# Two stages of deformable convolution on one core: image rows in four quarters over 128 partitions, shifted copies made by DMA, and four gathered groups instead of five

## The reference

```
x = x + layer0(gn(x))        x = x + layer1(gn(x))      gn: 32 groups, so each channel of each image by its own mean and variance
layer0(v): offsets = conv3x3(v) (8 maps), logits = conv3x3(v) (4 maps), attn = softmax(logits)
           sampled_k = bilinear sample of v at (pixel + offset_k), k = 0..3
           y = proj(sum_k attn_k * sampled_k);  batch norm of y over both images;  gamma, beta;  GELU
layer1(v): offset = conv3x3(v) (18 maps), m = sigmoid(conv3x3(v)) (9 maps)
           sample v (padded by one) at the nine taps of a 3x3 kernel, each shifted by its own offset, times m
           out = conv over the nine taps (32 -> 32 channels)
```

## Time and profile before

| what | value |
|---|---|
| median of three runs | 551.7 us (552.7, 551.7, 546.88) |
| span of the profiled execution | 551.0 us |
| what lies around the span, to the median | 0.7 us |
| PE, DVE, POOL, ACT busy | 83%, 78%, 69%, 37% |
| start, to the first window tile weighted | 0 to 44.6 us |
| loop of layer zero | 44.6 to 157.8 us |
| from there to the first interpolation of layer one | 157.8 to 204.9 us |
| layer one | 204.9 to 551.0 us |

### The profile page before, as it was taken

How to read it: one execution, slowest core, us unless ns; L and a number is a source line. 1 busy time by engine, 2 the same in 40 slices (tenths; PEclk the granted TensorE clock), 3 DMA queues, 4 the chain that set the end, 5 groups by cost and what they waited for, 6 DMA issues and landing times.

```text
span 551.0 us, 10909 instructions
## 1 busy us (share of the span) xinstructions
PE 459.4 (83%) x3913; PEld 261.4 (47%) x3913; DVE 429.5 (78%) x934; ACT 206.5 (37%) x352; POOL 379.0 (69%) x356
## 2 busy tenths in 40 slices
PE   5848888996750767989999999999899998899884
PEld 2527556665530522445555555555444444444443
DVE  5995667997759766788888879898787887779672
ACT  2714546321248556652433332333133142232201
POOL 6067656788827466577777777777777777777772
PEclk9756878998995756999999999999999999989999
DMA  8569747869500491122223227512112211212211
GB/s 201 180 154 202 192 89 125 158 114 157 124 18 0 158 119 46 37 68 73 74 72 91 70 73 110 86 49 54 54 54 58 58 49 54 58 49 56 55 49 32
DMA packets 43093, 48.48 MB, mean 88 GB/s; under 512 B 24482, under 2 KB 33954, under 8 KB 42532
## 3 DMA queue, kind: packets, MB, share of 16 engines
q1 hardware_dynamic: 32148, 25.52, 22.7%
q0 software_dynamic: 10752, 22.04, 15.9%
q10 hardware_dynamic: 144, 0.24, 0.2%
HBM read 39.02 MB, written 8.75 MB: 87 GB/s over the span
## 4 chain that ended last, share of the span: by engine, by line
PE 35%; POOL 25%; issue 15%; DVE 8%; DMA 8%; ACT 6%; SPq 1%; POOLq 1%; DVEq 0%; ACTq 0%
POOL got L570 23%; PE ps_later L1193 4%; PE ps_pair L1193 4%; DMA got<-table,idx 4%; PE ps_x L1206 4%; PE ps_raw L1169 4%; ACT xn L654 3%; DMA raw<-in_x 3%; PE ps_raw L983 3%; PE ps_x L1216 2%; PE ps_o L996 2%; POOL xn L555 1%; PE ps_pair L1042 1%; PE ps_later L1020 1%; SPq L445 1%
## 5 line engine op out<-in xcount | busy, mean ns | idle before, releaser
L570 POOL DMA_INDIRECT got<-table,idx x336 | 352.4, 1049 | 143.8 <-issue 109.7
L1811 DVE TENSOR_TENSOR prod<-got,wgt 128x512 f32<-128x512 f32 x64 | 44.2, 690 | 30.2 <-DMA got<-table,idx 29.8
L1612 DVE TENSOR_TENSOR vprod<-ps_pair,rhat 128x704 f32<-128x704 f32 x64 | 56.8, 887 | 9.7 <-PE ps_pair L1193 9.3
L1206 PE MATMUL ps_x<-early,vprod 128*128 128x128 f32 x384 | 56.3, 284 | 1.0 <-DVE vlast L1623 0.6
L1612 DVE TENSOR_TENSOR vprod<-ps_later,rhat 128x704 f32<-128x704 f32 x64 | 56.5, 882 | 0.9 <-PE ps_later L1193 0.8
L1206 PEld LDWEIGHTS ps_x<-early,vprod 128*128 128x128 f32 x384 | 42.4, 145 | 30.6 <-issue 17.3
L1620 DVE TENSOR_TENSOR vprod<-vprod 128x640 f32<-128x640 f32 x64 | 52.8, 825 | 1.2
L1794 DVE TENSOR_TENSOR samples<-shared,vprod 128x800 f32<-128x800 f32 x44 | 43.0, 984 | 12.2 <-PE ps_pair L1042 4.9
L1216 PE MATMUL ps_x<-early,prod 128*128 128x128 f32 x256 | 39.3, 277 | 10.5 <-DVE prod L1811 10.3
L654 ACT ACTIVATE xn<-raw,aff 32x1472 f32<-32x1472 f32 (+6 forms) x24 | 43.0, 1802 | 13.6 <-DVE aff L1394 9.4
L1169 PE MATMUL ps_raw<-conv_out,later 128*128 128x512 f32 x64 | 39.7, 704 | 0.7 <-ACT shared L827 0.7
(11 more groups left out here) (204 smaller groups left out, 776.3 us busy)
## 6 DMA issues: line engine op xcount, KB each, us to landing
shared<-positions SPq DMA_DIRECT2D x22, 440.0 KB
got<-table,idx POOLq DMA_INDIRECT x336, 6.0
raw<-in_x SPq DMA_DIRECT2D x16, 256.0 KB, 10.1
table<-trow SPq DMA_DIRECT2D x16, 256.0 KB, 2.0
y<-table SPq DMA_DIRECT2D x4, 512.0 KB, 8.6
table<-trow SPq DMA_DIRECT2D x4, 504.0 KB
out<-ysumT SPq DMA_DIRECT2D x64, 16.0 KB
later<-in_later SPq DMA_DIRECT2D x1, 530.0 KB, 18.9
```

Of the source, the lines that this page charges most:

```text
L570: pool.indirect_dma_start(into[t][:, s * P:(s + 1) * P], None, tab, bass.IndirectOffsetOnAxis(ap=idx[:, slot, k:k + 1], axis=0),).then_inc ...
L1206: nc.tensor.matmul(bank[:, P:2 * P], vprod[:, t % 2, r, :], idn[:], start=(r == 0), stop=(r == HALF - 1), is_transpose=True)
L1612: nc.vector.tensor_tensor(dst, ps_dense[pair_number(0, t, pair) % 2][:].rearrange("p (d n) -> p d n", d=2)[:, :, 0:WROWS * C].rearrange("p ...
L1811: nc.vector.tensor_tensor(prod[:, t % 2, :].rearrange("p (k s c) -> p s k c", k=CORNERS, c=C), got[t].rearrange("p (s k c) -> p s k c", s= ...
```

## The change

`raw` now holds an image once: row quarter q (16 rows, and the row below it) on partitions 32q to 32q+31. The steps that follow from it:

- `load_x`: four transfers an image instead of eight. Statistics and the residual sum work on 128 partitions and 1024 columns an image; a matmul with a rotated identity (`combine`) brings the four quarters' statistics to every partition.
- `normalise` is one DVE instruction an image into `xq` (quarters, padded); 16 transfers of 32 partitions an image (`load_shifted`) make the four shifted copies in `xn`. The first rows of group 0 are written directly by ACT and DVE (`head`). The row above a quarter comes by a matmul (`turn_edge`, `normalise_edge`).
- Tables: four 128x128 transposes make one of 8 (layer zero) or 9 (layer one) pieces; the table of layer zero goes out in two sends, that of layer one in three and three small ones (image 1: nine and three).
- Layer zero gathers four groups (16 steps) and takes twelve as windows, three tiles a step. One PSUM bank each for the gathered and the window sums. `fold_y` adds into PSUM banks that hold four groups by quarter, with the bias put there by a matmul (`start_y`); the copies to `y0` are gone, statistics and GELU read PSUM. Four GELUs instead of sixteen.

The core of the diff:

```diff
-NGA = 5
+NGA = 4
+GATHERED = [(0, 2 * i) for i in range(NGA)]
-UNITS = [[(0, 5), (0, 6)], [(0, 7)], [(1, 0), (1, 1)], [(1, 2), (1, 3)], [(1, 4), (1, 5)], [(1, 6), (1, 7)]]
+UNITS = [[(0, 1), (0, 3)], [(0, 5), (0, 7)], [(1, 0), (1, 2)], [(1, 4), (1, 6)], [(1, 1), (1, 3)], [(1, 5), (1, 7)]]
-CONV_AT = {(0, 0): [5], (1, 0): [6], (1, 1): [7], (2, 0): [8], (3, 1): [9], (4, 1): [10], (5, 1): [11], (6, 1): [12],
-           (7, 1): [13], (9, 1): [14], (10, 1): [15]}
+CONV_AT = {(0, 0): [6], (0, 1): [7], (1, 0): [8], (2, 0): [9], (2, 1): [10], (5, 0): [11], (6, 0): [12], (6, 1): [13],
+           (8, 0): [14], (8, 1): [15]}
...
+            def load_shifted(b, q, skip=0):
+                for g in range(CORNERS):
+                    dy, dx = g // 2, g % 2
+                    n = (QROWS - skip) * WP - dx
+                    src, dst = (1 + skip) * WP + dx, (1 - dy + QROWS * q + skip) * WP
+                    sp.dma_start(xn[C * g:C * (g + 1), b, dst:dst + n],
+                                 xq[C * q:C * (q + 1), b, src:src + n]).then_inc(xn_in[b][q], 16)
...
+            for q in range(Q):
+                load_shifted(0, q, 0 if q else HEAD)
+                if q % 2:
+                    send_corners(0, HALVES[q // 2], tab_copied, tab_out["00"])
             send_pixels(0)
...
+            sp.wait_ge(norm_xq, 2)
+            for q in range(Q):
+                load_shifted(1, q)
...
-            send(table[1][0], trow, CHUNKS, NT, tab_copied, tab_out["10"])
+            sp.wait_ge(norm_xq, 3)
+            load_shifted(0, 0, HEAD)
+            load_shifted(0, 1)
+            for k, ts in enumerate(SENT):
+                if k == 1:
+                    load_shifted(0, 2)
+                    load_shifted(0, 3)
+                sp.wait_ge(tab_copied, NT + ts.stop)
+                send_rows(table[1][0], ts, tab_out["10"])
+            send_last_rows(table[1][0], tab_out["10"])
             load_columns(0)
+            sp.wait_ge(norm_xq, 4)
+            for q in range(Q):
+                load_shifted(1, q)
...
+            def combine(n, a, z, bank):
+                pe.wait_ge(stats_in, n)
+                m = 6 * (z - a)
+                for q in range(Q):
+                    last = nc.tensor.matmul(bank[:, q * m:(q + 1) * m], wheel[:, C * q:C * q + P],
+                                            stats[:, a:z, :].rearrange("p j n -> p (j n)"), start=True, stop=True)
+                last.then_inc(stats_mm, 1)
...
             def fold_y(k, i):
+                b, j, q = y_place(k, i)
                 pe.wait_ge(ysumT_copied[k], i + 1)
-                if i >= 1:
-                    pe.wait_ge(y_copied[k], i)
-                nc.tensor.matmul((ps_x[2] if k == 0 else ps_o)[:, :], fold_of[y_index(k, i) // GB][:], ysumT[:, k, :], start=True,
+                if i % Q == 0:
+                    start_y(b, j)
+                nc.tensor.matmul(y_bank[j][C * q:C * (q + 1), :], fold_of[b][:], ysumT[:, k, :], start=False,
                                  stop=True).then_inc(y_mm[k], 1)
...
+            for j in range(2 * B):
+                nc.scalar.activation(yq[:, j, :], y_bank[j], ACT.Gelu, bias=aff[:, 2, 1:2],
+                                     scale=aff[:, 2, 0:1]).then_inc(gelu, 1)
...
+            def normalise(l, b):
                 dve.wait_ge(affine, AFFINE[l, b])
+                dve.wait_ge(pads_zero, PADS["xq"])
+                nc.vector.tensor_scalar(inside(b), pixels(b), aff[:, b, 0:1], aff[:, b, 1:2],
+                                        ALU.mult, ALU.add).then_inc(norm_xq, 1)
...
+            def add_layer0(b):
+                for h in range(2):
+                    j = 2 * b + h
+                    dve.wait_ge(gelu, j + 1)
+                    view = raw[:, b, h * GPIX:(h + 1) * GPIX]
+                    nc.vector.tensor_tensor(view, view, yq[:, j, :], ALU.add).then_inc(added, 1)
+                for h in range(2):
+                    dve.wait_ge(added, 2 * b + h + 1)
+                    last = statistics(b, h)
+                last.then_inc(stats_in, 1)
```

842 lines of the change are left out of this document (378 added, 464 removed).

## The result

The changed kernel takes 570.2 us, median of 4 runs (566.8 to 576.4), against 551.8 us for the kernel before, median of 4 runs beside it: ratio 1.034, 95% interval 1.028 to 1.040. It is slower, and lies above the whole of the forecast's range (526 to 558). Now and then an execution of any of these kernels runs slower at no fault of the program; the medians hold such executions, the ratios and intervals leave them out. The profiled execution took 566.8 us, with a span of 564.9 us at a mean granted clock of 0.905, as before.

A forecast was written before the change was run, and what follows sets the result against it. It took DVE to bound the start, PE and DVE the loop, then a chain of small steps and DMA between layers. Terms -4.8 - 1.3 - 1.0 = -7.1 from a span of 551.0 gave 543.9, predicted as 544 us, range 526 to 558.

The forecast's parts named there:

- The start: Up to the first window tile: first window load issued near 35.3 us, tile weighted near 42 us instead of 44.63.
- the price by bytes: DMA queue in the start: shifted copies at 201 GB/s, 9.2 us for image 0 and 10.4 for image 1.
- The third window load: Steps 1 and 2: issued behind image 1's pixels at 63 us against 57.15, landing 10 us later at 73.
- The rest of the loop: After nine window tiles: DVE 71 us, PE 74, with waits 80; loop ends at 153 us instead of 157.8, -4.8 us.
- the one sum bank: Loop: PE waits for ACT's copy at group changes, up to 1.2 us at ten places, half covered: 6 us.
- Between the layers: Loop's end to layer one's first interpolation: transposes come 11.5 us sooner, but copies delay the table, leaving -1.3 us.
- Layer one: Group 1's wait for ACT's normalisation goes, -1.0 us; nothing counted for group 0 or the extra sends and copies.
- Window loads pace the loop: Rival, chance 0.20: late window loads make a window cost 2.4 us; loop ends at 167, total 558 us.
- The DMA queue is no bound: Rival, chance 0.22: copies run at 259 GB/s or faster and overlap the sends; loop ends near 146, total 528 us.
- The two rules of the Trainium skill: DMA: 32-partition copies reach 8 of 16 ports, 9.7 us an image; 117-partition sends split 13 ways, about 1.7 us more.

The follow-up runs named there:

- e1_memset: Changed kernel with GpSimd clearing image 1's buffer before the first inverse root instead of after it; 572.3 us, ratio 1.035 to the kernel before.
- e4_third: Changed kernel with the third group's window load issued ahead of the send of image 1's pixels; 564.0 us, ratio 1.019 to the kernel before.
- e5_order: e4_third with image 1's shifted copies, later weights and column loads also reordered in SP's queue; 558.7 us, ratio 1.013 to the kernel before.
- e3_banks: Changed kernel with window sums of groups 2, 4, 6 and 8 in a second PSUM bank; 568.2 us, ratio 1.028 to the kernel before.
- e9_three: Changed kernel with a third product buffer for the window tiles and nothing else; 563.8 us, ratio 1.024 to the kernel before.
- c3_three: c2_early plus a third product buffer for the window tiles; 538.7 us, ratio 0.977 to the kernel before.
- c2_early: Changed kernel with nine edits: earlier memset, statistics, weights, pixels and turnings, two sum banks, third load and copies reordered, table sends first; 545.6 us, ratio 0.991.
- e10_before3: The kernel before the change, with a third product buffer added; 553.0 us, ratio 1.001 to the kernel before.
- e11_loop: Changed kernel with four loop edits (two sum banks, early third window load, reordered copies, third product buffer), start unchanged; 553.0 us, ratio 1.003.
- e8_nocopy: Changed kernel without image 1's 16 shifted-copy transfers (2.1 MB) in layer zero; 568.5 us, ratio 1.030 to the kernel before.
- e6_warm: e1_memset plus five filler matmuls on PE before convolution 7, where it waits for a shifted copy; 573.4 us, ratio 1.042.

## Why the prediction was wrong

- **The start.** I had the queue start at 15 us and issue the first window load at 35.3. It started at 19.49 and issued the load at 39.81: 20.3 us from one to the other, as forecast (19.5 to 20 in the other profiles with this start), so the price by bytes held there and the 4.5 us are the late start. 3.2 of them are the memset beside DVE's heads (I had "DVE starts at 12.0 us as now", "then two heads and the instruction", and did not look at what the change had put on POOL at that moment); e1_memset starts the copies at 16.30 and issues the load at 35.9. Then the load took 9.5 us to the first tile where I had 6.7, while the queue moved 140 GB/s (39.8 to 49.3 us) and not 201; that is the rest of the 7.3 us at this mark.
- **The third window load: the step that failed first.** I saw that "SP waits for those pixels before it issues the third window load" and put it at 63 us. The chain in front of it I let end at 57 us, plus 5; it ended at 61.5, 4.5 us late like the start, where PE got the copy that it had waited 2.9 us for, and 11.4 us passed from there to the send: two convolutions, three window sums, a wait of 1.41 us for the sum bank, the first bias and fold, a gathered sum, the transposes, ACT's copy. The mechanism was right, the size was off by 10 us. From the issue to the ninth tile 9.65 us passed, where I had 10. The worth of the late load is 6 us (e4_third), with the copies moved as well 11.5 (e5_order).
- **The rest of the loop: the step that failed most.** The term of -4.8 us at the loop's end came out at +19.3 (177.1 against 157.8); of the 24 us between, 10 lie before the ninth tile and 14 behind it, where I had 80 us and 94.1 passed. I added up DVE's work (71) and PE's (74), which was close (66.5 and 77.8), and put 6 us on top for the one sum bank. That takes the two engines as if they ran freely beside each other. They hand over tile by tile through two buffers, and the change had removed the DVE work and the gathered tiles that used to lie between the tiles. The sum of one engine's work is a lower bound for such a loop and not its time. The bank, which I did price, costs under 4 us (e3_banks); the product buffers, which I didn't look at since neither kernel changes them, cost some 6 (e9_three; 7 in c3_three against c2_early) and nothing in the kernel before (e10_before3). The two don't simply add up: with both mended and the order too (e11_loop) the stretch takes 87.9 us, 6.2 less and not 10. The late load is no part of these 14 us: without it (e4_third) the stretch still takes 93.4. In c3_three it takes 84.1; the 4 us left above my 80 no run explains. In my count of tiles, too, one window and one gathered tile were missing: 40 and 14 lie between the two marks, not 39 and 13.
- **Between the layers.** The first transposes were to come 13 us after the last sum and come 17.3 after it. 3.1 us of it lie before the first GELU (9.1 us against 5.9 today): PE's `combine` waits 3.70 us for DVE's queue at L1896, where I had counted "nothing". In the code DVE evaluates a branch (L1876) between its last statistics and that signal; that the branch is the cause is not tested. The table then was late for the reason that I named, the copies between its sends, and by more: 37.2 us from the loop's end to the column loads against 34 to 34.5. That the 11.5 us shrink to next to nothing was right.
- **Layer one.** -1.0 forecast, -7.2 measured (338.9 us from the first interpolation to the end against 346.1; in the other changed kernels it takes 337 to 345). 2.0 us at group 1 are there (19.64 between the convolutions of groups 0 and 1 instead of 21.6), 1.1 us are lost again behind it, and 6.3 us lie in group 0, where I counted nothing: in the kernel before, ACT's 8.18 us of normalisation stood ahead of a copy for which PE waited too. PE's timeline in the kernel before, its busy time in group 0 (columns as above), and then that of the changed kernel:

```profile
213.81 1.33 PE L996 MATMUL ps_o<-early,conv_out 128*128 128x27 f32 x8 [3.01 <-ACT conv_out L683]
```

```profile
204.93:230.15 25.22, 20.88 (x128) 8.59 (x128) 15.16 (x34) 17.19 (x16) 15.25 (x17) 0.74 0.16 45
```

```profile
225.99:244.95 18.96, 16.74 (x129) 7.14 (x129) 14.86 (x34) 5.05 (x10) 12.88 (x14) 0.92 0.67 151
```

The wait of 3.01 us is gone, and the same matmuls (128 and 129) keep PE busy for 4.1 us less, at a granted clock of 0.92 instead of 0.74.
- **The rivals.** "Window loads pace the loop" gave the right length for the loop behind the ninth tile (94 us) by the wrong mechanism: in the changed kernel one tile waits 7.6 us for a load that was issued late, and all others together 1.6 us for a transfer. That is luck. Its loop's end (167) was still 10 us early. "The DMA queue is no bound" is neither right nor wrong: taking 2.1 MB out of the queue gained 1.7 us (e8_nocopy), so the bytes by themselves were hardly a bound, while their order was one of 11.5 us. None of my rivals had order as its mechanism.
- **The two rules of the Trainium skill.** On copies cut by 32 partitions the page gave an estimated 9.7 us an image. No run shows their rate alone: sixteen were issued in 13.26 us while the queue moved 222 GB/s of copies, loads and gathers together; and e8_nocopy shows that this price hardly reached the time. The other, a transfer split 13 ways for 117 partitions, no run here shows by itself. (By the rule the estimate was 8.1 x 3/13 = 1.9 us, and not 1.7.)

**What stays open.** Whether a filled wait helps on average (e6_warm: the profile says yes, the times don't). What the last 4 us of the loop above my forecast are. Why PE's clock comes back after the wait in one execution and not in another. And how much of c3_three's start is each edit's: I ran them together.

## What to carry to other kernels

When a change takes work off an engine, look for what used to lie between its hand-overs: two product buffers were enough with the old work between the tiles and cost some 6 us without it, and an experiment on the kernel before (no gain there) is what shows that this belongs to the change. In an in-order queue, ask of each transfer which of the ones ahead of it it really needs: moving a load ahead of a send, and copies to where they are first read, brought 11.5 us here, where taking the bytes away brought 1.7. And a fix whose mechanism shows in the trace but not in the time is not refuted: it may be hidden by a later wait, so mend the last wait first and try again.

## What the hardware showed that I had not expected

- DVE's two writes of 32x640 take 1.24 us alone and 4.44 us when a GpSimd memset of 128x4356 (13.85 to 17.57 us) runs; the first of them took 3.80 us and ended 0.35 us behind the memset. The Trainium skill (SBUF — State Buffer, section SBUF: two separate sides) says that the port pair shared by VectorE, in a mode that uses two ports, and GpSimd is under "an **exclusive lock**, not a bandwidth split". By that rule, if the write is in such a mode (no run shows its mode), it is blocked until the memset's end, and the trace agrees.
- The same program had PE at a granted clock of 0.89 in one execution and 0.58 in another from 60 to 76 us, after a wait of 2.92 us in the one and 3.50 in the other, and the ninth tile 5.3 us apart.
- A transfer of 132 KB from 32 partitions to 32 others costs SP 0.83 us of issue when the queue is busy (16 in 13.26 us), and lands 3.0 us after it in the median. But the one that PE waited for at 61.53 us had been issued at 50.3 to 51.1: a median landing says little of the copy that matters.
